# A Mamba-2 and mixture-of-experts layer on one core: the scan's output and z laid out with channels in rows, the diagonal product in two column halves of the array, and six PSUM banks shared out anew

## What is computed

```python
q = apply_rope(x @ W_in[:256].T)              # 256 channels
zxbcdt = rmsnorm(q, norm_pre_w) @ W_zxbcdt.T  # z 512 | xBC 768 | dt 8
dt = softplus(dt + dt_bias)
xBC = silu(causal_conv4(xBC))                 # x_ssm 512, B 128, C 128
y = ssd(x_ssm, dt, A, B, C) + D * x_ssm       # 8 heads of 64 channels, state 128
y = rmsnorm(y * silu(z), norm_gated_w)
mixed = y @ W_out.T + q
x1 = x + layernorm(mixed)                     # then a layer norm, a router of 4 of 16 experts,
out = x1 + layernorm(experts(layernorm(x1)))  # 16 experts of width 64 and a shared one of 512
```

## Time and profile before

| | us |
|---|---|
| three runs: median (lowest to highest) | 3193.36 (3184.57 to 3193.8) |
| the profiled execution | 3187.6 |
| its span, first to last instruction | 3185.9 |

### The profile page before, as it was taken

One profiled execution on the slowest core, in us unless ns is written; L12 is line 12 of the kernel. 1 busy time (PEld: TensorE's weight loads), 2 busy tenths in 40 slices (PEclk: granted clock), 3 DMA queues, 4 the chain that ended last, 5 costly groups with the idle time before them and its releaser, 6 DMA issues.

```text
span 3185.9 us, 62383 instructions
## 1 busy us (share of the span) xinstructions
PE 3112.3 (98%) x19648; PEld 2722.1 (85%) x19648; DVE 2394.2 (75%) x5104; ACT 1935.2 (61%) x4149; POOL 2031.2 (64%) x2311
## 2 busy tenths in 40 slices
PE   5899999999999999999999999999999999999997
PEld 4688888888888888888888888888888888888886
DVE  5877877777777777777777777778777777777763
ACT  5565666665666556666566666656656656665562
POOL 2477666677666676656676666776666776666764
PEclk7899999999999999999999999999999999999999
DMA  3123222222222222222122222222222222222222
GB/s 123 41 68 87 73 73 67 66 66 85 73 64 64 71 73 76 80 66 58 64 86 76 76 60 66 66 86 73 73 66 66 66 86 73 64 67 69 73 74 48
DMA packets 143433, 227.33 MB, mean 71 GB/s; under 512 B 18976, under 2 KB 88352, under 8 KB 143392
## 3 DMA queue, kind: packets, MB, share of 16 engines
q1 hardware_dynamic: 126496, 210.06, 20.1%
q0 software_dynamic: 16896, 16.78, 4.0%
HBM read 174.87 MB, written 35.13 MB: 66 GB/s over the span
## 4 chain that ended last, share of the span: by engine, by line
PE 95%; DVE 0%; POOL 0%; ACT 0%; issue 0%; ACTq 0%; DVEq 0%; POOLq 0%
PE fpb L1443 34%; PE apb L1443 20%; PE acc L1629 17%; PE apb L1575 7%; PE apb L1452 4%; PE ppb L1443 3%; PE apb L1560 3%; PE apb L1567 2%; PE ppb L1462 2%; PE apb L1547 1%; PE fpb L1492 1%; PE fpb L1462 1%; PE fpb L1494 1%; PE fpb L1608 0%; PE apb L1520 0%; PE apb L1519 0%
## 5 line engine op out<-in xcount | busy, mean ns | idle before, releaser
L652 POOL TENSOR_TENSOR hidL<-hid,hidH 128x512 fp32r<-128x512 f32 x384 | 544.9, 1419 | 234.8 <-ACT hidH L914 226.8
L1130 DVE SCALAR_TENSOR_TENSOR xc<-apb,cw,xc 128x511 f32<-128x511 f32 (+2 forms) x576 | 427.8, 747 | 63.9 <-ACT xc L827 35.9
L1629 PE MATMUL acc<-WDH,hidH 128*128 128x256 f32 x1536 | 456.7, 297 | 4.4 <-POOLq L654 4.4
L914 ACT CAST hidH<-hid 128x512 fp32r<-128x512 f32 x384 | 236.2, 615 | 341.9 <-POOL hid L647 283.6
L1629 PE MATMUL acc<-WDH,hidL 128*128 128x256 f32 x1536 | 431.4, 281 | 0.0
L1629 PE MATMUL acc<-WDL,hidH 128*128 128x256 f32 x1536 | 430.9, 281 | 0.0
L647 POOL TENSOR_TENSOR hid<-hid,cb 128x512 f32<-128x512 f32 x256 | 347.5, 1358 | 73.2 <-DVEq L1251 42.1
L1249 DVE TENSOR_TENSOR hid<-hid,fpb 128x512 f32<-128x512 f32 x384 | 261.1, 680 | 135.6 <-PE fpb L1443 132.3
L1443 PE MATMUL fpb<-fTh,UH 128*128 128x512 f32 x768 | 335.7, 437 | 0.0
L845 ACT ACTIVATE seg<-seg,acs 128x128 f32<-128x128 f32 x1024 | 313.6, 389 | 11.5 <-ACT cb L895 5.7
L1443 PE MATMUL fpb<-fTh,GH 128*128 128x512 f32 x768 | 318.6, 415 | 0.0
(11 more groups left out here) (195 smaller groups left out, 8669.6 us busy)
## 6 DMA issues: line engine op xcount, KB each, us to landing
seg<-acs_row SPq DMA_DIRECT2D x128, 512.0 KB, 4.2
cb<-c_row SPq DMA_DIRECT2D x512, 128.0 KB, 2.9
xsP<-in_x SPq DMA_DIRECT2D x32, 512.0 KB, 3.6
xc<-qrot SPq DMA_DIRECT2D x32, 512.0 KB, 3.4
xc<-in_x SPq DMA_DIRECT2D x32, 512.0 KB, 4.3
out<-xc SPq DMA_DIRECT2D x32, 512.0 KB, 3.0
out<-xn POOLq DMA_DIRECT2D x32, 512.0 KB, 6.0
ZL_loaded<-in_wzx_t SPq DMA_DIRECT2D x2, 512.0 KB, 4.4
```

Source lines behind the costliest of these rows:

```text
L652: own.do(G.tensor_tensor(hidL[:, j % 2, :], hid[:, j % 2, :], hidH[:, j % 2, :].bitcast(fp32), ALU.subtract))
L914: A.copy(hidH[:, j % 2, :], hid[:, j % 2, :]).then_inc(sem["hidden_high"], 1)
L1130: ins = V.scalar_tensor_tensor(xc[:, b, s:], src[:, 0:T - s], cw[:, b, TAPS - 1 - s:TAPS - s], xc[:, b, s:], ALU.mult, ALU.add)
L1629: ins = nc.tensor.matmul(dst, l[:, w, tk], r[:, j, :], start=j == 0 and t % 2 == 0 and n == 0, stop=j == HB - 1 and n == 2, skip_group_che ...
```

## The change

- z is projected with channels in rows: weights ZH and ZL, hT moving, 24 matmuls over 512 tokens. dt gets its own small weights DTW (high and low part side by side) and 16 narrow matmuls (`project_dt`, by the helper `narrow` of the router's logits).
- `from_state` and `diagonal` swap weights and moving operand, so the scan's output has channels in rows. A head has 64 channels; even heads write partitions 0 to 63, odd heads 64 to 127, and the weights stand in the matching half of the array's columns.
- The decay exp(Acs) is now needed along a row: SyncE loads it from DRAM in two transfers (`own_rows`), ScalarE takes exp (`row_exp`). The buffer `own_decay` shares memory with xTh and xTl, so `evac_xT` waits for `chunk_y(2)`.
- The transposes of y go. `evac_y` and `y_low` read `zs` in SBUF; yTh and yTl are single buffers, with waits for the end of project_out. The fill `yT` leaves the ring.
- The sum of squares of a token now runs across partitions: ScalarE squares, VectorE adds four blocks to one in two steps (`sum_squares`), TensorE multiplies with a column of ones (`squares_by_token`), VectorE takes the sums (`squares_out`).
- xD comes from the convolved x in SBUF and a column of D (`dcol`).
- `apb` has two banks, `fpb` three. All lists of steps and the table of fills are written anew.

```diff
-        apb = [ctx.enter_context(nc.psum_tensor(f"apb{n}", [P, T], fp32)) for n in range(3)]
+        apb = [ctx.enter_context(nc.psum_tensor(f"apb{n}", [P, T], fp32)) for n in range(2)]
         ppb = [ctx.enter_context(nc.psum_tensor(f"ppb{n}", [P, T], fp32)) for n in range(1)]
-        fpb = [ctx.enter_context(nc.psum_tensor(f"fpb{n}", [P, T], fp32)) for n in range(2)]
+        fpb = [ctx.enter_context(nc.psum_tensor(f"fpb{n}", [P, T], fp32)) for n in range(3)]
...
-                ins = G.tensor_tensor(zs[:, c, :], zs[:, c, :], xD[:, c % 2, :], ALU.mult)
+                gate = zs[:, :, c * P:(c + 1) * P]
+                ins = G.tensor_tensor(gate, gate, xD[:, c % 2, :].rearrange("p (j n) -> p j n", j=NB), ALU.mult)
...
             def evac_xT(s):
                 way.filled(act, "ACT", f"xT{s}")
+                act.wait_ge(sem["xT_free"], 1)
...
-                free("a", name, A.activation(zs[:, c, n * DI // 2:(n + 1) * DI // 2], way.bank(name)[:, 0:DI // 2], ACT.Silu))
+            def silu_z(j):
+                way.filled(act, "ACT", f"z{j}")
+                free("a", f"z{j}", A.activation(zs[:, j, :], way.bank(f"z{j}")[:], ACT.Silu))
+            def row_exp():
+                act.wait_ge(sem["ear_loaded"], 32)
+                A.activation(own_decay[:], own_decay[:], ACT.Exp).then_inc(sem["ear_ready"], 1)
...
-                way.filled(act, "ACT", f"yT{c}")
-                A.copy(yTh[:].rearrange("p j n -> p (j n)"), way.bank(f"yT{c}")[:]).then_inc(sem["yh_ready"], 1)
+                act.wait_ge(sem["yg_ready"], c + 1)
+                if c == 2:
+                    act.wait_ge(sem["out_begun"], 1)
+                elif c:
+                    act.wait_ge(sem["yT_read"], (c + 1) // 2)
+                A.copy(yTh[:], zs[:, :, c * P:(c + 1) * P]).then_inc(sem["yh_ready"], 1)
             def square_y(c):
+                act.wait_ge(sem["yg_ready"], c + 1)
                 if c >= 2:
-                    own.wait()
-                ins = A.activation(junk[c % 2], zs[:, c, :], ACT.Square, accum_out=ssy[:, c:c + 1])
-                if c % 2:
-                    ins.then_inc(sem["ssy_ready"], 1)
-                else:
-                    own.mark(ins)
+                    act.wait_ge(sem["sq_summed"], 1)
+                A.activation(junk[c % 2].rearrange("p (j n) -> p j n", j=NB), zs[:, :, c * P:(c + 1) * P], ACT.Square
+                             ).then_inc(sem["sq_ready"], 1)
...
-                free("a", f"xt{c}", V.tensor_tensor(by_head(xD[:, c % 2, :]), by_head(way.bank(f"xt{c}")[:]),
-                                                    along(dbc[:]), ALU.mult))
+                ins = V.tensor_tensor(by_block(xD[:, c % 2, :]), xc[:, 0:NB, c * P:(c + 1) * P],
+                                      dcol[:].unsqueeze(2).broadcast_to([P, NB, P]), ALU.mult)
+                if c == NT - 1:
+                    own.do(ins)
+                    dve.sem_inc(sem["xc_read"], 1)
+                    dve.sem_inc(sem["xs_free"], 1)
+                    free("a", f"xt{c}")
+                else:
+                    free("a", f"xt{c}", ins)
...
-                free("a", f"yT{c}", V.tensor_tensor(yTl[:].rearrange("p j n -> p (j n)"), way.bank(f"yT{c}")[:],
-                                                    yTh[:].rearrange("p j n -> p (j n)").bitcast(fp32), ALU.subtract))
+                V.tensor_tensor(yTl[:], zs[:, :, c * P:(c + 1) * P], yTh[:].bitcast(fp32),
+                                ALU.subtract).then_inc(sem["yl_ready"], 1)
+            def sum_squares(c):
+                dve.wait_ge(sem["sq_ready"], c + 1)
+                q = junk[c % 2]
+                own.do(V.tensor_tensor(q[:, 0:2 * P], q[:, 0:2 * P], q[:, 2 * P:4 * P], ALU.add))
+                V.tensor_tensor(q[:, 0:P], q[:, 0:P], q[:, P:2 * P], ALU.add).then_inc(sem["qs_ready"], 1)
+            def squares_out(s):
+                way.filled(dve, "DVE", f"ss{s}")
+                own.do(V.tensor_copy(ssy[:, pair(s)], way.bank(f"ss{s}")[:, 0:2]))
+                free("a", f"ss{s}")
+                if s == 0:
+                    dve.sem_inc(sem["sq_summed"], 1)
+                dve.sem_inc(sem["ssy_ready"], 1)
...
-            def project_z(c, n):
-                name, tk = f"z{'ab'[n]}{c}", slice(c * P, (c + 1) * P)
-                cs = slice(DI // 2 + HS, ZC) if n else slice(0, DI // 2 + HS)
-                b = slot(name)
-                if c == 0 and n == 0:
-                    pe.wait_ge(s_hT, 2)
-                    pe.sem_inc(s_hT, -2)
-                fill(name, split_mm(b[:, 0:cs.stop - cs.start], [(hTh[:, k, tk], hTl[:, k, tk], ZH[:, k, cs], ZL[:, k, cs])
-                                                                 for k in range(KD)],
-                                    sem["hT_read"] if c == NT - 1 and n == 1 else None))
+            def project_dt():
+                b = slot("dt")
+                pe.wait_ge(s_hT, 2)
+                pe.sem_inc(s_hT, -2)
+                fill("dt", narrow(b, hTh, hTl, DTW, HS))
+            def project_z(j):
+                name, lo = f"z{j}", j * P + (HS if j >= NB // 2 else 0)
+                cs = slice(lo, lo + P)
+                fill(name, split_mm(slot(name)[:], [(ZH[:, k, cs], ZL[:, k, cs], hTh[:, k, :], hTl[:, k, :])
+                                                    for k in range(KD)], sem["hT_read"] if j == NB - 1 else None))
...
-                fill(f"yo{c}", nc.tensor.matmul(b[:], xc[:, 5, c * P:(c + 1) * P], S[:], start=True, stop=True))
+                for j in range(NB):
+                    js = slice(j * P, (j + 1) * P)
+                    ins = nc.tensor.matmul(b[:, js], S[:, js], xc[:, 5, c * P:(c + 1) * P], start=True, stop=True)
+                fill(f"yo{c}", ins)
...
-                    hs = slice(h * PD, (h + 1) * PD)
-                    ins = nc.tensor.matmul(b[:, hs], seg[:, c % 2, h, :], xdt[:, c % 2, hs], start=True, stop=True)
+                    half = slice(h % 2 * PD, (h % 2 + 1) * PD)
+                    ins = nc.tensor.matmul(b[half, h // 2 * P:(h // 2 + 1) * P], xdt[:, c % 2, h * PD:(h + 1) * PD],
+                                           seg[:, c % 2, h, :], start=True, stop=True)
                 fill(f"yd{c}", ins)
-            def y_by_channel(c):
-                b = slot(f"yT{c}")
-                pe.wait_ge(sem["yg_ready"], c + 1)
-                fill(f"yT{c}", transposes(b, lambda j: zs[:, c, j * P:(j + 1) * P], NB))
+            def squares_by_token(s):
+                b = slot(f"ss{s}")
+                for n in range(2):
+                    c = 2 * s + n
+                    pe.wait_ge(sem["qs_ready"], c + 1)
+                    ins = nc.tensor.matmul(b[:, n:n + 1], junk[n][:, 0:P], ones[:, 0:1], start=True, stop=True)
+                fill(f"ss{s}", ins)
             def project_out(t):
                 s = t // 2
                 b = way.bank(f"out{s}") if t % 2 else slot(f"out{s}")
-                read_out(f"yT{t}")
-                ins = split_mm(b[:, (t % 2) * D:(t % 2 + 1) * D], [(yTh[:, j, :], yTl[:, j, :], WOH[:, j, :], WOL[:, j, :])
-                                                                   for j in range(NB)])
+                pe.wait_ge(sem["yl_ready"], t + 1)
+                ins = split_mm(b[:, (t % 2) * D:(t % 2 + 1) * D],
+                               [(yTh[:, j, :], yTl[:, j, :], WOH[:, j, :], WOL[:, j, :]) for j in range(NB)])
                 if t % 2:
                     ins.then_inc(sem["out_ready"], 1)
+                else:
+                    ins.then_inc(sem["yT_read"], 1)
...
```

482 lines of the change are left out of this document (245 added, 237 removed).

## The result

The change makes the kernel slower: 3289.61 us (median of four runs, 3285.36 to 3291.15) against 3189.96 us beside it (four runs, 3184.57 to 3193.8), ratio 1.031 with a 95% interval of 1.029 to 1.033. The profiled execution took 3288.9 us, 101.3 more than the one before, and lies far above the forecast of 3176 us and above the range's end, 3264.

The account below looks back on a forecast made before the run. TensorE was taken as the bound, waiting for nearly nothing in 96.40 us turns. 3187.6 + 28 (matmuls) - 49 (diagonal) + 10 (waits) = 3176.6, stated as 3176 us; 8-in-10 range 3155 to 3264 us.

Parts of the forecast that it names:

- 1 to 5, matmuls that come and go: TensorE: transposes removed, z, dt, state output and squares changed; together +0.87 us per sequence, +28 us over 32.
- 6, the diagonal: Diagonal on two column halves side by side: nine slots for 16, 1.35 us a visit against 1.73, -49 us.
- The edges: Around a diagonal visit: each change of division about 0.095 us, plus unhidden weight loads, 0.055 us in and 0.107 out.
- Rivals A and B: Diagonal: A, halves do not overlap, 3263 us, chance 0.26; B, they overlap but loads wait, 3217 us, chance 0.14.
- 7 and 8, the waits: Fewer scan PSUM banks and new waits on y: bounds 0 and 1.5 us per sequence, taken as 0.3, +10 us.
- one tight place, project_out(3): Wait for y's low part at chunk 3's output projection: TensorE's cover 1.86 us against a chain of 1.74 us.
- the row's median: Stretching of VectorE operations with two SBUF operands: wait taken nearer L1219's median of 477 ns than its maximum, 1514.
- off the path, with cover: VectorE's 8 small adds and some stretching, perhaps 82 of 96 us busy instead of 74, not added to the sum.
- Rival C: Halves overlap as forecast, but the waits last, at 1.2 us per sequence: 3205 us, chance 0.12.
- The bank of 7: Scan's PSUM ring with two banks in place of three: 2.7 us or more of other matmuls lie between uses.
- Lead, first and tail: Work outside the steady loop turns, reordered by the change: cost 0, within 5 us.

Follow-up runs that it names:

- e12: Kernel after, with GpSimd's add of the D product and gate multiplication on 2 columns in place of 512; 3176.0 us (one run).
- e6: Kernel after, with three banks in the scan's ring and the down projection's two sum banks made one; 3285.2 us (one run).
- e5: Kernel before, each head's tokens cut in two for the array's column halves, seg still the weights, y's layout kept; 3132.0 us, ratio 0.982.

## Why the prediction was wrong, point by point

**1 to 5, matmuls that come and go (+0.87 us a turn).** Borne out. Counted in instructions, -16 transposes, +16 for dt, -24 for z, +18 for the state, +8 for the squares are 2 more a sequence, 64 in all, as the pages count (19712 against 19648). And in e12, where TensorE waits for nothing, a turn is 95.15 us, where 96.40 + 0.87 - 4 x 0.52 gives 95.19.

**6, the diagonal (-49 us).** Right in mechanism, undersized: -0.52 us a visit in place of -0.38, since there are eight slots, not nine: the two halves start together, with their loads at once, so the slots take 8 x 0.109 = 0.87 us in place of 1.00. The edges came as forecast, 0.14 us going in (0.09, and 0.05 more between the first two pairs; forecast 0.15) and 0.20 coming out. Rivals A and B fall. The Trainium skill, TensorE: Matmul & The Clock Gate, Part 3, by which a load overlaps running matmuls only where row groups differ, does not hold for these column halves, whose loads start 0.007 us apart.

**7 and 8, the waits (+10 us taken, bounds 0 to 1.5 us a turn).** This is the step that failed, and it decides all. In e12's turn there are none; in the kernel after a turn is 98.57, so the waits are **3.42 us a turn**, more than twice the upper bound. From start to start against the same matmuls in e12, they are 0.63 us before state(2), 0.85 before the squares' product, 0.31 before the query, 0.93 before project_out(0) and 0.71 before project_out(2). (The list of waits gives 2.58 us a turn, as it counts only from the end of the matmul before.) There were three faults in the working. It looked for one tight place, project_out(3), where cover and chain were both counted. That one cost nothing; the waits stand at the five other places, where only VectorE's order was read and not how late it runs. It took the row's median for operations that meet GpSimd, "nearer the row's median of 477 than its maximum". Of the 128 subtractions for y's low part the mean is 1122 ns, not 690, and an add of 128 columns comes to 1222 in one of its two groups. And it costed the squares' adds as 8 small operations "off the path, with cover", while each chunk's stand between GpSimd's gate and x's low part in one queue. Rival C had this mechanism, at 1.2 us. The bank of 7 had no part in it (e6).

**The clock** was not in the sum: six long turns of 1.57 us, 9.4 us.

**Lead, first and tail (0, within 5 us).** They lost 29 us, the second miss. Half of it goes with the waits (in e12 first turn, last turn and the rest are 5, 5 and 5 us shorter). In the last stretch TensorE's clock is lower: behind the last cumulate, the kernel before and then the kernel after (PE, PEld, DVE, ACT, POOL, granted clock):
```profile
3040.50:3185.90 145.40, 123.51 (x757) 106.01 (x755) 67.74 (x150) 64.33 (x125) 85.56 (x88) 0.97 0.26 67
```
```profile
3125.50:3287.00 161.50, 134.67 (x787) 114.31 (x785) 82.02 (x175) 65.43 (x122) 88.25 (x89) 0.90 0.26 65
```
There are also 30 more matmuls there by the other order. How much is whose stays open; no run tried it.

The sum with these sizes: 29 x (-1.25) = -36, waits 29 x 3.42 = +99, clock +9.4, edges +29: +101 us, as measured. The sign of the forecast hung on a term of 3.4 us a turn that was taken at 0.3; e12, which has the change's whole TensorE work and in its loop none of the waits, runs in the 3176 us that were forecast. That this agrees to the microsecond is chance: e12's diagonal gains 18 us more than was forecast and it has none of the 10 us of waits, while its clock costs 9 us and its edges 18 that were not in the sum (14 lost, and 4 that their three sequences should have gained).

## What to carry to other kernels

Where TensorE is busy for 98% and waits for nothing, price a change first by what it adds to the queues that feed TensorE, at the durations that operations have *beside* GpSimd, and for every consumer in its order, not for the one tight place that comes to mind. Short VectorE operations with both operands in SBUF are not cheap there: each may last as long as the GpSimd operation next to it, even with two columns. And if a hardware feature is wanted (here the column halves), look for the form of it that leaves all layouts and other engines alone, as e5 does, before paying for a new layout.
